# A sort stage of a point network: points loaded before constants, a norm merged into its block, and its side work re-timed

## The reference, cut to what matters

```python
xn = (x - mean(x, -1)) / sqrt(var(x, -1) + 1e-5)
q = clip(floor((coords - cmin) * 1023 / (cmax - cmin + 1e-6)), 0, 1023)   # coords: first 3 rows of the context, per batch
keys = [morton(q), morton(q[y, x, z]), hilbert(q), hilbert(q[y, x, z])]   # 30 bits each
orders = [argsort(k, axis=1) for k in keys]
# hilbert, for each bit Q from the highest down to 2, P = Q - 1, for each axis i:
cond = X[i] & Q > 0
t = (X[0] ^ X[i]) & P
X[0] = where(cond, X[0] ^ P, X[0] ^ t);  X[i] = where(cond, X[i], X[i] ^ t)   # X[i] only for i > 0
# much later: k = context @ Wk, v = context @ Wv (512 x 128 each, per batch)
```

## Time and profile before

| what | us |
| --- | --- |
| median of 3 runs | 1141.55 |
| the profiled execution, its own time | 1143.61 |
| its span, first to last instruction | 1141.9 |
| busy: TensorE matmul / VectorE / ScalarE / GpSimd | 925.4 / 742.7 / 455.5 / 360.7 |
| from the span's start to the sort's last instruction | 130.1 |

### The profile page before, as it was taken

The page is one execution under the profiler, slowest core; times in us unless marked ns, Lnnn a source line. Parts: engine busy times, 40 slices in busy tenths (PEclk is TensorE's granted clock), DMA queues, the critical chain, the costliest instruction groups (busy, mean ns, idle before and its releaser), DMA issues. The chain is left out here.

```text
span 1141.9 us, 27535 instructions
## 1 busy us (share of the span) xinstructions
PE 925.4 (81%) x10896; PEld 652.0 (57%) x10896; DVE 742.7 (65%) x1891; ACT 455.5 (40%) x1009; POOL 360.7 (32%) x272
## 2 busy tenths in 40 slices
PE   1891396888779699995499999949977799985898
PEld 1661254555445477674299999846425555642675
DVE  5899696998889399998423232364433389854542
ACT  0889675753328465332022222230002277750100
POOL 0000128999641689892200000000000365510000
PEclk9996597999969899997699999959999799997899
DMA  4765333121053864820244545314435548501000
GB/s 132 280 202 183 81 83 82 42 58 33 14 115 102 146 82 68 97 52 1 59 138 138 161 142 151 98 57 160 148 112 178 212 167 316 173 17 37 1 1 19
DMA packets 134084, 123.77 MB, mean 108 GB/s; under 512 B 30521, under 2 KB 108153, under 8 KB 132434
## 3 DMA queue, kind: packets, MB, share of 16 engines
q1 hardware_dynamic: 133314, 117.97, 38.0%
q10 hardware_dynamic: 656, 4.23, 0.9%
HBM read 109.84 MB, written 12.32 MB: 107 GB/s over the span
## 5 line engine op out<-in xcount | busy, mean ns | idle before, releaser
L577 POOL TENSOR_TENSOR stage_diff<-win_ext,win_F 128x960 f16<-128x960 f32 x88 | 165.9, 1887 | 44.7 <-DVE stage_hi L732 41.2
L1074 ACT ACTIVATE attend_prob<-attend_centred 124x480 f32<-124x480 f32 x88 | 52.2, 594 | 129.0 <-DVE attend_centred L1117 129.0
L1318 DVE TENSOR_SCALAR attn_qT<-proj_qp,attn_bq,attn_gq 128x256 f32 x32 | 17.4, 544 | 121.9 <-ACT attn_sq L1297 121.9
L986 POOL TENSOR_TENSOR attend_pnorm<-attend_prob,attend_inv 124x480 f32<-124x480 f32 x88 | 87.1, 990 | 21.2 <-DVE attend_inv L1130 20.9
L763 PE MATMUL order_ordered<-stage_hi,stage_lo 128*32 128x512 bf16 x528 | 52.4, 419 | 49.9 <-DVE stage_hi L732 48.6
L1110 DVE TENSOR_REDUCE attend_top<-attend_score 124x32 f32<-124x480 f32 x88 | 55.7, 633 | 35.8 <-PE attend_score L1020 35.5
L1048 PE MATMUL attend_outp<-stage_FX,stage_WX 128*64 128x240 f32 (+3 forms) x352 | 74.5, 387 | 0.5 <-issue 0.5
L1032 PE MATMUL attend_prob_t<-core_ident,attend_pnorm 124*128 124x124 f32 x344 | 57.0, 288 | 14.0 <-POOL attend_pnorm L986 13.9
L1020 PEld LDWEIGHTS attend_score<-stage_hi,stage_diff 128*60 128x60 f16 x1376 | 48.8, 112 | 30.7 <-issue 24.7
L1061 PEld LDWEIGHTS attend_outp<-attend_probT,stage_vT 64*32 64x32 f32 (+1 forms) x2752 | 45.5, 122 | 36.2 <-ACT attend_probT L1081 25.5
L763 PEld LDWEIGHTS order_ordered<-stage_hi,stage_lo 128*32 128x32 bf16 x528 | 23.8, 101 | 73.2 <-ACT stage_lo L838 44.3
(11 more groups left out here) (331 smaller groups left out, 2212.5 us busy)
## 6 DMA issues: line engine op xcount, KB each, us to landing
binary_base<-in_fmean_dram SPq DMA_DIRECT2D x8, 1344.0 KB, 8.7
cross_raw<-in_fw_dram SPq DMA_DIRECT2D x24, 448.0 KB, 7.0
sort_ctxT<-in_ctxT_dram SPq DMA_DIRECT2D x8, 1024.0 KB, 8.0
attn_wq<-in_Wq_dram SPq DMA_DIRECT2D x32, 256.0 KB, 2.9
attn_wk<-in_Wk_dram SPq DMA_DIRECT2D x32, 256.0 KB, 3.3
attn_wv<-in_Wv_dram SPq DMA_DIRECT2D x32, 256.0 KB, 3.6
att_wo<-in_Wo_dram SPq DMA_DIRECT2D x32, 256.0 KB, 2.6
stage_vT<-scratch_values SPq DMA_DIRECT2D x64, 120.0 KB, 5.3
```

What stands on the lines that cost most here:

```text
L577: return nc.gpsimd.tensor_tensor(out[:, :, 0:size], spread, f.unsqueeze(3).to_broadcast([P, QB, size, WIN]), ALU.subtract)
L986: nc.gpsimd.tensor_tensor(pnorm[g % 2][:, 0:n, 0:K].rearrange("p r (h w) -> p r h w", w=SPAN), prob[g % 3][:, 0:n * HEADS].rearrange("p (r ...
```

## The change

- Loads: phase_setup is gone. In the sort's block SyncE issues pts, ident and x first, then goes on with the context; the other six constants are issued after the last store, and the block waits for them. ScalarE's queue loads the rows of the minima, ahead of all else there. Each load has a semaphore of its own. The memset of "ones" goes to GpSimd.
- The first norm has no block of its own: the statistics stand on VectorE behind low_wide, the Sqrt on ScalarE ahead of move_keys, the scalings on VectorE behind the copy of keyT[0], the turns on TensorE ahead of the first product, the copies of xnT on VectorE at the second bit of the exchange and on ScalarE ahead of row 0.
- keyT[0] is copied right behind make_bounds(0), no longer within the exchange.
- The exchange has 6 instructions instead of 7 for axes 1 and 2.
- Context copies on ScalarE stand behind rows 1, 4, 7, 11, 15, 19, 23 and 27.
- SyncE's loop is unrolled, and move_keys(sp, 1) stands behind store 3, ahead of load 6. VectorE waits for the second turn and copies keyT[1] before row 1. TensorE's order of turn and products stays.
- The turned minima and keys share one PSUM bank.

```diff
-CONSTANTS = ("ident", "iota", "headmask", "rowsof", "mask", "mask0", "kvmask")
+CONSTANTS = ("iota", "headmask", "rowsof", "mask", "mask0", "kvmask")
...
-def phase_setup(nc, T, D):
...
+LATE_KEYS = 3
+CONTEXT_ROWS = (1, 4, 7, 11, 15, 19, 23, 27)
...
-        for u in range(2):
-            load(u, u)
-        with sp.Fori(0, B // 2 - 1) as j:
-            for u in range(2):
-                sp.wait_ge(self.made, j * 2 + (u + 1))
-                load(j * 2 + (u + 2), u)
-                sp.wait_ge(self.copied, j * 2 + (u + 1))
-                store(j * 2 + u, u)
-        between(sp)
-        for b in range(B - 2, B):
+        for b in range(2):
+            load(b, b)
+        for b in range(B):
+            if b + 2 < B:
+                sp.wait_ge(self.made, b + 1)
+                load(b + 2, b % 2)
             sp.wait_ge(self.copied, b + 1)
             store(b, b % 2)
+            if b == LATE_KEYS:
+                between(sp)
...
-        def load_points(sp):
-            for c in range(3):
-                sp.dma_start(rows[c * B:(c + 1) * B, :], D["ctx_4096"][:, c, :]).then_inc(loaded, 16)
-            sp.dma_start(pts[:], D["pts"].rearrange("p (c t) -> p c t", t=KC)).then_inc(loaded, 16)
-
-        phase_layernorm(nc, T, "ln0", load_points)
...
@@ -308,15 +296,22 @@
             @block.sync
             def _(sp):
+                sp.dma_start(pts[:], D["pts"].rearrange("p (c t) -> p c t", t=KC)).then_inc(points_in, 16)
+                sp.dma_start(T["ident"][:], D["ident"]).then_inc(ident_in, 16)
+                sp.dma_start(T["x"][:], D["x"].rearrange("b c n -> (b c) n").rearrange("(t p) n -> p t n", p=P)).then_inc(x_in, 16)
 
                 def late_keys(sp):
                     move_keys(sp, 1)
                 context.move(sp, late_keys)
+                for name in CONSTANTS:
+                    sp.dma_start(T[name][:], D[name]).then_inc(constants_in, 16)
+                sp.wait_ge(constants_in, 16 * len(CONSTANTS))
...
@@ -326,11 +321,17 @@
+                pe.wait_ge(ident_in, 16)
                 pe.wait_ge(low_ready, 1)
...
                 turn_keys(0)
+                for t in range(RT):
+                    pe.wait_ge(xn_ready, t + 1)
+                    for c in range(KC):
+                        mm = nc.tensor.transpose(xn_turned[t][:, c * P:(c + 1) * P], T["xn"][:, t, c * P:(c + 1) * P], T["ident"][:])
+                    mm.then_inc(xn_turn, 1)
                 context.multiply_first(pe)
                 context.multiply_others(pe, 2, B - 2)
                 turn_keys(1)
@@ -338,7 +339,13 @@
             @block.scalar
             def _(act):
+                for c in range(3):
+                    act.dma_start(rows[c * B:(c + 1) * B, :], D["ctx_4096"][:, c, :]).then_inc(rows_in, 16)
+                act.wait_ge(var_ready, 1)
+                nc.scalar.activation(std[:], var[:], ACT.Sqrt).then_inc(std_ready, 1)
                 move_keys(act, 0)
+                act.wait_ge(xn_turn, 2)
+                nc.scalar.copy(T["xnT"][:, :, P:2 * P], xn_turned[1][:].rearrange("p (c r) -> p c r", c=KC))
...
-                    if row % 2 == 1 and row // 2 < B:
-                        context.evacuate(act, row // 2)
+                    if row in CONTEXT_ROWS:
+                        context.evacuate(act, CONTEXT_ROWS.index(row))
...
-                dve.wait_ge(loaded, 64)
+                dve.wait_ge(rows_in, 48)
...
                 vec.tensor_copy(low_wide[R], low[R].unsqueeze(2).to_broadcast([3 * B, 2, P])).then_inc(low_ready, 1)
+                statistics()
+                dve.wait_ge(points_in, 16)
                 dve.wait_ge(low_turned, 1)
...
                 make_keys(0)
                 make_bounds(0)
+                dve.wait_ge(turned, 1)
+                vec.tensor_copy(keyT[0][:], keyP[0][:]).then_inc(keyT_ready, 1)
+                normalised()
...
-                        if bit == NUM_BITS - 1 and a == 1:
-                            dve.wait_ge(turned, 1)
-                            vec.tensor_copy(keyT[0][:], keyP[0][:]).then_inc(keyT_ready, 1)
-
+                        if bit == NUM_BITS - 2 and a == 0:
+                            dve.wait_ge(xn_turn, 1)
+                            vec.tensor_copy(T["xnT"][:, :, 0:P], xn_turned[0][:].rearrange("p (c r) -> p c r", c=KC))
                         go(vec.tensor_scalar(flip[:], X[a], 31 - bit, 31, ALU.logical_shift_left, ALU.arith_shift_right))
-                        if a:
-                            go(vec.tensor_tensor(diff[:], X[0], X[a], ALU.bitwise_xor))
-                            go(vec.tensor_scalar(turn[:], flip[:], low_bits, low_bits, ALU.bitwise_and, ALU.bitwise_xor))
-                            go(vec.tensor_tensor(diff[:], diff[:], turn[:], ALU.bitwise_and))
-                            go(vec.tensor_tensor(X[a], X[a], diff[:], ALU.bitwise_xor))
-                            go(vec.tensor_tensor(X[0], X[0], diff[:], ALU.bitwise_xor))
-                        go(vec.scalar_tensor_tensor(out=X[0], in0=flip[:], scalar=low_bits, in1=X[0],
+                        if not a:
+                            go(vec.scalar_tensor_tensor(out=X[0], in0=flip[:], scalar=low_bits, in1=X[0],
+                                                        op0=ALU.bitwise_and, op1=ALU.bitwise_xor))
+                            continue
+                        go(vec.tensor_tensor(diff[:], X[0], X[a], ALU.bitwise_xor))
+                        go(vec.tensor_tensor(diff[:], diff[:], flip[:], ALU.bitwise_or))
+                        go(vec.scalar_tensor_tensor(out=X[0], in0=diff[:], scalar=low_bits, in1=X[0],
+                                                    op0=ALU.bitwise_and, op1=ALU.bitwise_xor))
+                        go(vec.tensor_tensor(turn[:], diff[:], flip[:], ALU.bitwise_xor))
+                        go(vec.scalar_tensor_tensor(out=X[a], in0=turn[:], scalar=low_bits, in1=X[a],
                                                     op0=ALU.bitwise_and, op1=ALU.bitwise_xor))
...
-                    if row == B // 2:
+                    if row == 1:
                         dve.wait_ge(turned, 2)
                         vec.tensor_copy(keyT[1][:], keyP[1][:]).then_inc(keyT_ready, 1)
...
-        phase_setup(nc, T, D)
```

More of the change, by code:

```diff
@@ L95, in sem @@
         return handle
-def phase_setup(nc, T, D):
-    with Scope(nc, "setup") as s:
-        loaded = s.sem("loaded")
-        with nc.Block() as block:
-            @block.sync
-            def _(sp):
-                sp.dma_start(T["x"][:], D["x"].rearrange("b c n -> (b c) n").rearrange("(t p) n -> p t n", p=P)).then_inc(loaded, 16)
-                for name in CONSTANTS:
-                    sp.dma_start(T[name][:], D[name]).then_inc(loaded, 16)
-                sp.wait_ge(loaded, 16 * (1 + len(CONSTANTS)))
-            @block.vector
-            def _(dve):
-                nc.vector.memset(T["ones"][:], 1.0)
 def phase_layernorm(nc, T, name, early=None):
@@ L282, in phase_sort @@
         earlier = s.sb("earlier", [P, P])
-        keyP = [s.ps(f"keyP{h}", [HALF, P]) for h in range(2)]
-        lowP = s.ps("lowP", [P, 2, 3 * B])
+        small = s.ps("small", [P, N])
+        keyP = [small[0:HALF, h * P:(h + 1) * P] for h in range(2)]
+        lowP = small[:, 2 * P:2 * P + 6 * B].rearrange("p (a b) -> p a b", b=3 * B)
         (step, low_ready, low_turned, key_ready, keyT_ready, turned, keys_out, lstep, earlier_ready) = (
@@ L319, in _ @@
                 nc.gpsimd.memset(earlier[:], 2.0 ** -100).then_inc(lstep, 1)
+                nc.gpsimd.memset(T["ones"][:], 1.0)
                 pool.wait_ge(lstep, 2)
@@ L371, in _, with statistics, normalised @@
                 R = slice(0, 3 * B)
-                dve.wait_ge(loaded, 64)
+                lgo = Steps(dve, lnstep)
+                def statistics():
+                    dve.wait_ge(x_in, 16)
+                    for t in range(RT):
+                        lgo(vec.bn_stats(stats[:, t, :], T["x"][:, t, :]))
+                        lgo(vec.bn_aggr(mv[:, t, :], stats[:, t, :]))
+                    vec.tensor_scalar(var[:], mv[:, :, 1], 1e-5, None, ALU.add).then_inc(var_ready, 1)
+                def normalised():
+                    dve.wait_ge(std_ready, 1)
+                    lgo(vec.reciprocal(rstd[:], std[:]))
+                    refine_rsqrt(vec, lgo, rstd[:], var[:], room[:])
+                    for t in range(RT):
+                        vec.tensor_scalar(T["xn"][:, t, :], T["x"][:, t, :], mv[:, t, 0:1], rstd[:, t:t + 1],
+                                          ALU.subtract, ALU.mult).then_inc(xn_ready, 1)
+                dve.wait_ge(rows_in, 48)
                 go(vec.tensor_reduce(low[R, 0:1], rows[R, :], AX.X, ALU.min))
```

15 lines of the change are left out of this document (12 added, 3 removed).

## The result

The changed kernel takes 1136.1 us, the median of 20 runs (1131.6 to 1139.7), against 1141.5 us for the kernel before on the same chips. The ratio of the two, taken over all the runs, is 0.9944, with a 95% interval from 0.9928 to 0.9959: 6.4 us less, 4.7 to 8.2. (The two medians alone differ by 5.4.) That is faster, and by less than the 1% that the prediction took for the least that a measurement can tell. The forecast was 9.4 us less (1132.2). It lies 3.9 us too low, inside the range and outside its own narrower one, and even the interval's best end, 8.2, doesn't reach 9.4.

The account below looks back on a forecast made before the run. The sort's end was taken to be set by the chain up to ScalarE's first row and ScalarE's 95.2 us behind it. 8.1 + 1.3 = 9.4 us off 1141.55 gave 1132.2 us, range 1128.5 to 1138.0, its own 1130.5 to 1134.5.

Parts of the forecast that it names:

- Part 1: Chain from the first loads to ScalarE's first row in the sort: that row comes 8.1 us earlier.
- S: Start of ScalarE's first row in the sort: 34.0 us before the change, forecast at 25.9.
- Part 2: ScalarE's rows and copies behind its first row: 6.8 us of waits traded for 6.0 at row 16, 1.3 less.
- It ends at S + 93.9: End of ScalarE's 32 rows, counted from its first row, against S + 95.2 before: 1.3 us less.
- copy 6: Context copy behind row 23: product 6 ready only just in time, up to 1.7 us may be lost.
- The first rival, product 5 at full clock: TensorE ahead of the second turn: turn 1.8 us sooner, gain 11.2 us, 1130.4 us; chance 0.21.
- Part 3: VectorE's shorter exchange: 4.1 us less work that buys nothing, about 7.2 us idle at the wait for the second turn.
- Part 4: Constants issued after the last store, at the sort's end: taken as nothing, 1.9 us as the other bound.
- the slow key store: Second keys' store on SyncE still costs 7.6 us: gain shrinks to 3.6, 1138.0 us; chance 0.14 with late loads.
- keys in time: Row 16 does not wait for the second keys: another 6.0 us, gain 15.4, 1126.2 us; chance 0.04.
- products at half clock throughout: TensorE ahead of the second turn: products take up to 14 us instead of 7.0, time 1167; chance 0.04.
- The sum: Whole kernel: 8.1 + 1.3 = 9.4 us less, from the median 1141.55 to 1132.2 us.

Follow-up runs that it names:

- experiment 3: Kernel before with all of the change but the start: spread copies, sooner second keys, wait before row 1, shorter exchange; old setup and norm; 1145.15 us, ratio 1.0034.
- old exchange: Changed kernel with the seven-instruction exchange of the kernel before, 18 instructions more; one time of 1128.87 us.
- loop kept: Changed kernel with the loop kept on SyncE for stores 0 to 3, same order of transfers; ratio 0.9951.
- start only: Changed kernel with copies behind odd rows, keys' store after store 5, VectorE's wait before row 4 and the seven-instruction exchange put back; 1137.2 us, ratio 0.9949.
- early turn, loop kept: Changed kernel with TensorE's second turn of keys ahead of product 5 and the loop kept on SyncE; ratio 0.9912.
- Experiment 1: Changed kernel with one edit, TensorE's second turn of keys ahead of product 5 instead of behind it; 1131.45 us, ratio 0.990.

## Why the prediction was right or wrong

**The start (Part 1).** The mechanism is right and the size nearly. The forecast had the minima at 4.7, the store at 19.0, S at 25.9; the profile of the changed kernel has 3.81, 17.88 and 24.05. The first load landed 3.0 us after its issue and not 3.2 behind the third issue, 0.9 less (in all nine profiles with this start the minima begin between 3.81 and 4.69, so the 4.7 was the upper end); the chain from minima to store took 14.1 where I had 14.3; and the store and first broadcast took 6.2 where I had carried 6.9 over. In nine profiles with this start S lies between 24.05 and 25.31, mean 24.8; in the four with the old one between 32.94 and 34.03, mean 33.4. So the start is worth 8.6 us on average, against the 8.1 of the forecast and the 10.0 that the single pair shows.

**Behind S (Part 2).** The path to row 16 came out term by term. The gap ahead of product 5 was 3.12 us (3.4 forecast), its length to the turn 8.75 (8.8), the store 1.8, row 16 at S + 53.2 (53.3) after 5.9 us of waiting (6.0). The Trainium skill ("DMA: Bandwidth & Descriptors", section on queues, rings and completion order) says that each DMA engine takes a ring's descriptors in their order. The trace agrees: the same store on the same queue took 4.7 to 7.6 us behind a 1 MB load (7.6 in the earlier trace rows) and 1.8 to 2.8 without one, and load 6, behind four 1 MB broadcasts, 14.6.

The step that failed is the end of this part, "It ends at S + 93.9", and the term is copy 6. I had seen that product 6 would be "only just in time", gave it up to 1.7 us and then left it at nothing in the sum. It cost 2.25 us, and E came at S + 96.3; with it taken away E would be at S + 94.0, next to the forecast. The forecast shows no working for product 6, and the low clock that it counted for product 5 it nowhere counts for product 6. That is what made the copy wait. TensorE stood idle for 18.84 us until load 6 landed, and product 6 then took 10.2 us, 3.2 more than the 7.0 of a product at full clock; ScalarE waited 2.25, so at full clock it would have been ready some 1 us ahead of the copy (an estimate from these rows). The same holds in each of the seven profiles in which load 6 stood behind the broadcasts and copy 6 waited: product 6, behind 12.4 to 19.0 us of idle time, took 8.9 to 10.2 us, and the wait, 0.8 to 2.3 us, was always shorter than what that is over 7.0. No run takes the dip away with load 6 as late, so this is read from rows and not tested by an edit. The 1.3 us that this part was to bring became -1.1 in this execution, 0.1 in experiment 3, and 2.3 in the two with the keys behind store 3, the turn behind product 5 and product 5 at full clock (E - S of 92.9).

**The first rival, product 5 at full clock,** held in some profiles. After the same idle 3.12 to 3.13 us, ahead of the same product released by the same copy, the eight matmuls took 5.34 and 5.37 us in two profiles (the changed kernel, experiment 3) and 3.67 in two others (old exchange, loop kept). These are four kernels with one profile each, so they don't show by themselves that one kernel does both. Two profiles of the kernel before do, for another product: product 0, behind the first turn and 8.66 and 8.65 us of idle time ahead of that, took 5.03 us for its first eight matmuls in the first profile and 6.43 in the second. The two rows, from the timelines of TensorE from 20 to 46 us:

```profile
25.74 5.03 PE L217 MATMUL sort_kp<-sort_ctxT,sort_wk 128*128 128x512 f32 x8
```

```profile
25.47 6.43 PE L217 MATMUL sort_kp<-sort_ctxT,sort_wk 128*128 128x512 f32 x8
```

I had weighed 0.57 against 0.21, as if one were true of every execution; more likely each is true of some. At E the two cases lie 3.4 us apart (96.3 against 92.9 behind S): 1.9 us less waiting at row 16 with the loop kept, about the 1.8 of the rival, and 1.5 us less at copy 6, where product 6 also started quicker.

**The exchange (Part 3).** Right, in both directions: 7.1 us of idle time at the new wait (7.2 forecast), no loss when the old exchange comes back (one profile), and 4.4 us (92.5 less 88.1) once the turn is early. VectorE's rows began at S + 37.9 (37.7), but ended 2.86 us ahead of ScalarE rather than within 1, since ScalarE was the later one by copy 6.

**Constants (Part 4).** Hidden, as taken: SyncE's last wait in its block is 3.7 us for the other engines, behind 1.4 for the constants. In the changed kernel neither the slow key store, nor keys in time, nor products at half clock throughout showed.

**The sum.** "The rest of the program starts on the ranks and is not touched. A gain in the sort goes straight into the time" is where the remainder failed. The sort's gain is 8.9 us in the first pair of profiles and 8.3 against the mean E of three (128.6, from the two profiles of the kernel before and its unrolled form). That it is near the 9.4 of the forecast is luck: more at the start, less behind it. The time fell by 6.4, 4.7 to 8.2. This table sets the same two numbers side by side for each kernel with many runs, in us less than the kernel before:

| kernel | E earlier than 128.6 | time shorter (95%) |
| --- | --- | --- |
| changed | 8.3 | 6.4 (4.7 to 8.2) |
| start only | 8.0 | 5.8 (3.3 to 8.4) |
| turn ahead of product 5 | 15.6 | 11.5 (7.4 to 15.4) |
| changed, loop kept | 10.7 | 5.6 (3.3 to 7.9) |
| early turn, loop kept | 15.1 | 10.1 (6.4 to 13.7) |
| all but the start | 0.5 | -3.9 (-6.1 to -1.8) |
| before, loop unrolled | 0.9 | -2.7 (-5.8 to 0.3) |

E is from one profile each and moves by some 3 us with the clock of products 5 and 6, so no single row proves a loss, but all lean the same way. What is shown: two profiles of one kernel differ by 2.8 us in the rest, and a stage that no edit touches takes 15.4 or 18.3 us with its clock. Two things speak against simple causes. Taking the loop back brought nothing in the changed kernel. And the mean granted clock of the span doesn't go with the missing time. Against the kernel before in the same batch of runs it is 0.9144 to 0.9138 in experiment 3 and 0.9160 to 0.9140 in the changed kernel with its loop kept, so not lower, though it is slightly lower in the start alone (0.9138 to 0.9149) and in the unrolled kernel before (0.9124 to 0.9140). Whether the clock's dips fall in costlier places when the sort ends earlier, or some other shared edit costs 2 to 4 us, stays open; the mean of the rest over 13 profiles (1.0 more, give or take 1.5) allows both.

**A better version.** Experiment 1 is faster than the kernel before, 0.990 of it [0.9865, 0.9935], and by its ratio than the changed one, 0.9944 [0.9928, 0.9959], though the two intervals just touch. The pair with the loop kept leans the same way (0.9912 and 0.9951), and so does E, 7.3 us earlier. It moves one line of TensorE's order.

## What to carry to other kernels

Where an engine's program is a written order, ask of each small step with a far reader (here a turn of 0.3 us, on which row 16 waits) what stands ahead of it and what that waits for: moving it ahead of one waiting product gave 7.3 us in the sort, more than re-timing the copies, the store and the exchange together. If two waits are close, take the smaller one out of the sum only when it is sure to be hidden; a wait called "just in time" behind four 1 MB transfers wasn't. If you price one product for a low clock after idle time, price each product that follows idle time so: product 6, after the longest idle time of all, was given no such price and took 3.2 us more than at full clock. And profile a kernel twice before you give a cause to 3 us anywhere in it.

## What the runs showed of the hardware

- The length of the idle time doesn't settle the clock of the next eight 128x512 matmuls. After 3.12 to 3.13 us of it they took 5.34 and 5.37 us in two profiles, with the granted clock at 0.50 in the window from 62 to 64 us of the first, and 3.67 in two others. Product 2 dropped after 2.01 us in the second profile of the kernel before (5.40 us) and held after 2.72 in experiment 3 (3.70 us). After 11.7 to 19.0 us, product 6 dropped in all eight profiles that have such a wait (5.45 to 6.77 us). The Trainium skill's page "TensorE: Matmul & The Clock Gate" (section on oscillation in real kernels) describes full and half clock in turn within a kernel, and the windows above agree.
- The same holds for a whole stage: 15.3 to 15.4 us in nine profiles, 18.2 to 18.3 in four, behind the same 0.52 us of idle time.
- A first load of 48 KB in three issues from 0.81 us on, alone on its queue, was read at 3.81 us in the changed kernel and between 3.81 and 4.69 in all nine profiles with this start, 3.0 to 3.9 us after the first issue.
